# A new order of the setup calls on each engine of an attention kernel

## The chip, the core and the metric

The kernel runs on one core of a Trainium2 chip. The engines are TensorE (PE, matmul and its weight load, PEld), VectorE (DVE), ScalarE (ACT), GpSimd (POOL) and SyncE (SP, which here only issues DMAs; ACT issues DMAs as well). Every engine takes its own instructions strictly in the order in which the program lists them; between engines there are semaphores. The metric is the time of one execution in device microseconds. Before the change: 723.69 us, median of 3 runs (722.16 to 724.40).

## The reference

```python
h = jnp.maximum(_layernorm(x), 0.0)              # x: 4096 x 256
q = h @ Wq.T + bq;  k = h @ Wk.T + bk;  v = h @ Wv.T + bv
a = q @ k.T * (1 / 16) + adj + adj               # 4096 x 4096
out = x + softmax(a, axis=-1) @ v
```

All inputs and the output are fp32. `adj` is 64 MB; it is read once.

## The kernel before

**Precision.** Each fp32 operand of a large product is split into a high and a low fp16 half, and three fp16 products (high x high, high x low, low x high) are summed in PSUM. A high half is a cast on ACT, a low half is a subtraction on DVE or POOL that waits for the high one.

**Scores.** q and k are folded: with M = Wq' Wk (Wq' the transpose) the scores are h M h', scaled, plus bias terms. `project_g(g, c)` makes the query side h M of group g (512 rows of h), feature half c, `evict_g` takes it from PSUM on ACT (one PSUM bank, so the next `project_g` waits for it), `store_g` and `load_g` carry it through a DRAM scratch to `g_pair`. Tiles are taken in pairs (256 rows) against blocks of 1024 keys (a quad q of 4), and each 2 x 2 block product is done with seven products instead of eight (a Strassen-like scheme): `product_1` to `product_7` read the combinations B11, B21, B22 (plain) and T1 to T4 (sums, made by `key_sum_t1` to `t4` on POOL out of `hf`). Their high halves are `high_key(q, i)` on ACT, their low halves `low_key` on DVE or `pool_low_key` on POOL; `LOW_ORDER` and `POOL_LOW_ORDER` say which engine makes which, and the semaphore values are looked up in these lists. DVE reads the results: `scores_11`, `scores_12`, `scores_22` (which also add the scaled adj rows) free the banks `t_ps[n % 2]` for the next product, and `finish_xx` add the second part and take the maximum.

**Values.** `project_v(unit)` (16 units) gives v for 256 rows; `high_v` (ACT) and `low_v` (DVE) write its halves, and `project_v(unit)` waits for `low_v(unit - 1)` since they share a bank. `move_v(g)` brings them with 4 DMAs to `v_sb`.

**Layernorm.** `load_x(g)` brings 512 rows; `statistics(g)` (DVE), `layernorm_factors(g)` (POOL) and four `normalise(g, k)` (ACT) make h; `transpose_h(g, c)` (PE) and `copy_h(g, c)` (ACT) lay it out by features.

**Softmax and weighing.** Per tile `bias` (DVE) gives the maximum, `exponential` (ACT) the weights, `turn` (DVE) and the exchanges `exchange_a` (8 DMAs from SP) and `exchange_b` (8 DMAs from ACT, in four calls of two) transpose them into `xT`; `high(m)` (ACT) and `low(m)` (POOL) split them, and `weigh` (PE) multiplies with `v_sb`. `refill(u, part)` loads the next adj row unit into the ring `rows` of 15 units once the exchange of that unit has landed; `load_rows(r)` does the first 15. `exchange_b(1, ...)` and `exchange_a(1)` wait by `arrival_free` until all products of v and g are through and `move_v(7)` has landed.

**Order.** The setup (up to period 7 of 64) is a list of calls written out by hand on each engine; from period 7 on loops run (`period(n)`), with four weighing parts and seven products in a period. Nothing else sets the order. The profile's line numbers are those of the functions: 1443 is a matmul of projections and weighing, 1504 a score product, 1064 `low_key`, 616 `pool_low_key`, 735 `high_key`, 709 `normalise`, 743 `evict_g`, 750 `high_v`, 1069 `low_v`, 545 `layernorm_factors`, 1046 `statistics`, 556 to 580 the key sums, 778 `exponential`, 789 `exchange_b`, 420 `exchange_a`, 372 the adj rows, 366 the x groups, 409 `move_v`, 391 `store_g`.

## Time and profile before

| | |
|---|---|
| median of 3 runs | 723.69 us |
| profiled execution, its own time | 720.62 us |
| its span, first to last instruction | 718.9 us |
| PE busy | 690.8 us (96%) |
| DVE busy | 603.4 us (84%) |
| ACT busy | 436.4 us (61%) |
| POOL busy | 432.9 us (60%) |
| DMA | 161.06 MB |

The span's clock starts at its first instruction. Busy shares over the whole span mix the setup (about the first 115 us) with the loop, so the stages have to be read apart. In a timeline row the bracket at the end is the idle time of that engine just before the row, and who ended it.

### The profile page before, as it was taken

What the parts mean: (1) busy time and instruction counts of PE and PEld (TensorE: products, weight loads), DVE (VectorE), ACT (ScalarE), POOL (GpSimd) and SP (SyncE); (2) the same over time, 40 slices, a digit from 0 to 9 for tenths busy, and PEclk for the clock granted to TensorE, in tenths of its full rate; (3) what the DMA queues carried; (4) which work ended last, traced back from release to release, by engine and by line L of the source; (5) the groups of instructions that cost most, each with busy time, mean ns of one, the idle gap of its engine ahead of it and who ended that gap; (6) DMA issues with size and microseconds to landing.
All of it is one profiled execution on the core that took longest, in us unless ns stands there. A gap on an engine that the chain in (4) does not pass through costs nothing.

```text
span 718.9 us, 14692 instructions
## 1 busy us (share of the span) xinstructions
PE 690.8 (96%) x4799; PEld 473.4 (66%) x4799; DVE 603.4 (84%) x1282; ACT 436.4 (61%) x732; POOL 432.9 (60%) x436
## 2 busy tenths in 40 slices
PE   4788999999999999999999999999999999999988
PEld 3555555567666667667667666666666666667766
DVE  4889777988897978788888888797988888888896
ACT  4799564665656555656656565656566666656530
POOL 1889603475655667474747556565738475655667
PEclk8799999999999999999999999999999999999999
DMA  8398588998879889898988897888879798878472
GB/s 284 119 279 234 142 223 224 258 252 229 251 207 258 223 230 232 237 240 226 269 208 246 235 254 217 241 216 243 239 217 266 205 256 231 250 217 225 121 187 75
DMA packets 93244, 161.06 MB, mean 224 GB/s; under 512 B 20976, under 2 KB 41840, under 8 KB 93168
## 3 DMA queue, kind: packets, MB, share of 16 engines
q1 hardware_dynamic: 68432, 126.41, 63.9%
q10 hardware_dynamic: 24736, 33.72, 18.3%
q8 instruction: 38, 0.62, 0.4%
q14 instruction: 38, 0.31, 0.2%
HBM read 80.35 MB, written 8.39 MB: 123 GB/s over the span
## 4 chain that ended last, share of the span: by engine, by line
PE 74%; DVE 10%; issue 4%; POOL 3%; DMA 2%; ACT 2%; ACTq 2%; SPq 1%; DVEq 0%; POOLq 0%
PE bank L1443 41%; PE bank L1504 33%; ACTq L789 2%; DVE rows L1128 2%; DVE rows L1101 1%; DMA xT<-rows 1%; DVE top L1137 1%; SPq L420 1%; DVE h_tile L1142 1%; POOL wT L625 1%; DVE stats L1046 1%; DVE rows L1094 1%; DMA rows<-in_x 1%; DMA g_pair<-g_scratch 1%; ACT rows L709 1%
## 5 line engine op out<-in xcount | busy, mean ns | idle before, releaser
L625 POOL TENSOR_TENSOR wT<-xT,wT 128x512 f16<-128x512 f32 x233 | 268.3, 1162 | 209.8 <-ACT wT L807 206.8
L1443 PE MATMUL bank<-v_sb,wT 128*128 128x256 f16 x2796 | 343.0, 273 | 0.2
L1504 PE MATMUL bank<-top,a_op 128*128 128x512 f16 x1344 | 330.8, 379 | 5.5 <-DVE chunk_max L1101 2.3
L1443 PEld LDWEIGHTS bank<-v_sb,wT 128*128 128x128 f16 x2796 | 273.3, 98 | 81.4 <-DVE xy L1191 1.3
L807 ACT CAST wT<-xT 128x512 f16<-128x512 f32 x233 | 139.6, 611 | 124.8 <-PE bank L1443 66.1
L1504 PEld LDWEIGHTS bank<-top,a_op 128*128 128x128 f16 x1344 | 130.6, 98 | 116.0 <-DVE chunk_max L1101 3.6
L778 ACT ACTIVATE rows<-rows,exp_bias,exp_scale 128x1024 f32<-128x1024 f32 x128 | 158.7, 1240 | 65.0 <-issue 31.0
L1101 DVE CUSTOM_DVE_ANT_0 rows<-bank,rows 128x512 f32<-128x512 f32 x256 | 173.6, 680 | 10.7 <-PE bank L1504 2.3
L1128 DVE STREAM_TRANSPOSE rows<-rows 128x1024 f32<-128x1024 f32 x128 | 158.3, 1239 | 5.8 <-ACT rows L778 5.5
L1086 DVE SCALAR_TENSOR_TENSOR rows<-rows,adj_scale,bank 128x512 f32<-128x512 f32 x64 | 47.7, 745 | 41.7 <-PE bank L1504 41.7
L769 ACT ACTIVATE rows<-rows,adj_scale 128x512 f32<-128x512 f32 x64 | 46.2, 722 | 36.0 <-POOL wT L625 20.7
L1079 DVE SCALAR_TENSOR_TENSOR rows<-rows,adj_scale,bank 128x512 f32<-128x512 f32 x64 | 47.5, 742 | 21.9 <-PE bank L1504 21.0
L1094 DVE SCALAR_TENSOR_TENSOR rows<-rows,adj_scale,bank 128x512 f32<-128x512 f32 x64 | 47.2, 737 | 8.4 <-PE bank L1504 8.3
L1443 PE MATMUL bank<-v_sb,top 128*128 128x256 f16 x276 | 31.5, 273 | 2.2 <-DVE top L1137 1.3
L1443 PEld LDWEIGHTS bank<-v_sb,top 128*128 128x128 f16 x276 | 25.6, 98 | 7.9 <-POOL top L625 1.9
L602 POOL TENSOR_TENSOR a_op<-g_pair,a_op 128x512 f16<-128x512 f32 x15 | 17.7, 1183 | 13.0 <-ACT a_op L763 13.0
L592 POOL TENSOR_TENSOR comb<-g_pair 128x128 f32<-128x128 f32 x15 | 6.8, 455 | 29.5 <-DMA g_pair<-g_scratch 29.5
L632 POOL TENSOR_TENSOR xy<-xy,bv_row 128x256 f32<-128x256 f32 x32 | 24.5, 769 | 0.0
L1443 PE MATMUL bank<-top,xT 128*128 128x512 f16 x72 | 19.4, 400 | 4.8 <-ACT xT L743 4.8
L778 ACT ACTIVATION_READ_ACCUMULATOR rows<-rows,exp_bias,exp_scale 128x1 f32 x128 | 23.9, 187 | 0.0
L1142 DVE CUSTOM_DVE_ANT_0 h_tile<-h_tile,wqbk_row,rbias 128x256 f32<-128x256 f32 x32 | 23.2, 726 | 0.1
L1443 PE MATMUL bank<-xT,top 128*128 128x256 f16 x144 | 19.9, 275 | 2.8 <-DVE xT L1069 1.7
(115 smaller groups left out, 478.8 us busy)
## 6 DMA issues: line engine op xcount, KB each, us to landing
rows<-in_adj SPq DMA_DIRECT2D x128, 512.0 KB, 5.9
xT<-rows SPq DMA_DIRECT2D x488, 64.0 KB, 3.2
xT<-rows ACTq DMA_DIRECT2D x488, 64.0 KB, 3.7
rows<-in_x SPq DMA_DIRECT2D x8, 512.0 KB, 5.5
xy<-in_x SPq DMA_DIRECT2D x32, 128.0 KB, 5.8
g_scratch<-xT SPq DMA_DIRECT2D x16, 256.0 KB, 3.4
g_pair<-g_scratch SPq DMA_DIRECT2D x15, 256.0 KB, 4.4
out_y<-xy SPq DMA_DIRECT2D x30, 128.0 KB, 5.7
```

The source lines that it names most:

```text
L625: nc.gpsimd.tensor_tensor(split_piece(m, 1), exchanged(m), split_piece(m, 0), ALU.subtract).then_inc(split_lo, 1)
L769: nc.scalar.activation(part, part, ACT.Copy, scale=adj_scale[:]).then_inc(adj_scaled, 1)
L778: nc.scalar.activation(row, row, ACT.Exp, scale=exp_scale[:], bias=exp_bias[:, p % 2, t:t + 1], accum_out=unit_sum(u, part)).then_inc(expe ...
L807: nc.scalar.copy(split_piece(m, 0), exchanged(m)).then_inc(split_hi, 1)
L1079: nc.vector.scalar_tensor_tensor(part, part, adj_scale[:], t_ps[n % 2][:], ALU.mult, ALU.add).then_inc(t_read[n % 2], 1)
L1086: nc.vector.scalar_tensor_tensor(part, part, adj_scale[:], t_ps[n % 2][:], ALU.mult, ALU.add).then_inc(t_read[n % 2], 1)
L1094: nc.vector.scalar_tensor_tensor(part, part, adj_scale[:], t_ps[n % 2][:], ALU.mult, ALU.add).then_inc(t_read[n % 2], 1)
L1101: return nc.vector.tensor_tensor_reduce(out=row, in0=ps[:], in1=row, scale=1.0, scalar=-3.0e38, op0=ALU.add, op1=ALU.max, accum_out=chunk_ ...
L1128: nc.vector.transpose(unit_row(u, part), unit_row(u, part)).then_inc(turned, 1)
L1142: nc.vector.tensor_tensor_reduce(out=h, in0=h, in1=wqbk_row[:], scale=SCORE_SCALE / H_SCALE, scalar=rbias0[:], op0=ALU.mult, op1=ALU.add, ...
L1443: return nc.tensor.matmul(out_ap, stationary, moving, start=first, stop=last)
L1504: last = nc.tensor.matmul(ps[:], s, mv, start=first and k == 0, stop=k == 2, skip_group_check=True)
```

## The change

It permutes calls within each engine's setup list; the loops and every function stay. One call changes its engine: the low half (0, B21) is made by `pool_low_key` instead of `low_key`. The order of the DMA issues on SP is changed too, and with it the order of the first adj rows (three of them now go ahead of x group 2, and x group 3 after the xy tiles). Blank lines that it removes are left out here, and the lines stand without their indentation.

The lists of which half comes when:

```diff
@@ -50,19 +50,19 @@
...
 HIGH_ORDER = (
-    (0, B11), (0, B21), (0, T1), (0, B22), (0, T3), (0, T2), (0, T4),
-    (1, B11), (1, B21), (1, T1), (1, B22), (1, T3), (2, B11), (1, T2),
-    (1, T4), (2, T1), (2, B21), (2, T3), (3, B11), (2, T2), (2, B22),
+    (0, B11), (0, B21), (0, T1), (0, B22), (0, T2), (0, T3), (0, T4),
+    (1, B11), (1, B21), (1, T1), (1, T3), (1, B22), (2, B11), (1, T2),
+    (1, T4), (2, B21), (2, T3), (2, T1), (3, B11), (2, T2), (2, B22),
     (3, B21), (2, T4), (3, B22), (3, T1), (3, T3), (3, T2), (3, T4),
...
 LOW_ORDER = (
-    (0, B11), (0, B21), (0, B22), (0, T4), (1, B11), (1, B21), (1, B22),
-    (2, B11), (2, B21), (3, B11), (2, B22), (3, B21), (3, B22),
+    (0, B11), (0, B22), (1, B11), (0, T4), (1, B21), (1, B22), (2, B11),
+    (3, B11), (2, B21), (2, B22), (3, B21), (3, B22),
 )
 POOL_LOW_ORDER = (
-    (0, T1), (0, T3), (0, T2), (1, T1), (1, T3), (1, T2), (1, T4),
-    (2, T1), (2, T3), (2, T2), (2, T4), (3, T3), (3, T2), (3, T1),
-    (3, T4),
+    (0, B21), (0, T1), (0, T2), (0, T3), (1, T1), (1, T3), (1, T2),
+    (1, T4), (2, T1), (2, T2), (2, T3), (2, T4), (3, T2), (3, T1),
+    (3, T3), (3, T4),
 )
...
```

SyncE, the order of issue:

```diff
@@ -435,67 +435,67 @@
...
 load_x(1)
+load_rows(0)
+load_rows(1)
+load_rows(2)
 load_x(2)
-load_x(3)
 sp.dma_start(bv_row[:], bv.rearrange("(o d) -> o d", o=1).to_broadcast([P, D])
              ).then_inc(bv_loaded, 16)
-load_rows(0)
-load_rows(1)
 load_xy(0)
...
 load_xy(3)
+load_x(3)
 load_x(4)
-load_rows(2)
+load_rows(3)
+load_rows(4)
 load_x(5)
-load_rows(3)
+load_rows(5)
+load_x(6)
 store_g(0)
-load_x(6)
-load_rows(4)
-load_rows(5)
 move_v(0)
-load_g(1)
 load_x(7)
...
 load_rows(8)
+load_g(1)
+move_v(2)
 sp.wait_ge(h_transposed, 12)
 load_rows(9)
-move_v(2)
 sp.wait_ge(h_transposed, 14)
 load_rows(10)
+move_v(3)
+store_g(1)
 low_keys(sp, 2, B11, B21, B22)
...
 load_rows(12)
-move_v(3)
-store_g(1)
+move_v(4)
 sp.wait_ge(h_transposed, 16)
 load_rows(13)
-move_v(4)
 store_g(2)
...
 store_g(4)
-move_v(6)
 refill(0, 0)
 store_g(5)
+move_v(6)
+move_v(7)
+store_g(6)
 sp.wait_ge(v_moved[0], 64 * (GROUPS // 2))
 load_rows(14)
-move_v(7)
-store_g(6)
-refill(0, 1)
 store_g(7)
 exchange_a(1)
+refill(0, 1)
 refill(1, 0)
+refill(1, 1)
 exchange_a(2)
-refill(1, 1)
...
```

GpSimd:

```diff
@@ -634,52 +634,53 @@
...
 layernorm_factors(1)
+pool_low_key(0, B21)
 key_sum_t1(0)
...
 key_sum_t2(0)
+layernorm_factors(2)
 key_sum_t4(0)
+layernorm_factors(3)
 pool_low_key(0, T1)
-layernorm_factors(2)
+pool_low_key(0, T2)
 pool_low_key(0, T3)
-layernorm_factors(3)
+query_sums(0)
 layernorm_factors(4)
-pool_low_key(0, T2)
-query_sums(0)
 layernorm_factors(5)
...
 layernorm_factors(6)
+key_sum_t2(1)
 pool_low_key(1, T1)
+key_sum_t4(1)
 pool_low_key(1, T3)
-key_sum_t2(1)
-key_sum_t4(1)
 pool_low_key(1, T2)
...
 key_sum_t2(2)
-key_sum_t4(2)
 layernorm_factors(7)
 pool_low_key(2, T1)
+pool_low_key(2, T2)
 pool_low_key(2, T3)
-pool_low_key(2, T2)
+key_sum_t4(2)
 query_sums(1)
+key_sum_t1(3)
 pool_low_key(2, T4)
-key_sum_t1(3)
 key_sum_t3(3)
 key_sum_t2(3)
-pool_low_key(3, T3)
 pool_low_key(3, T2)
 pool_low_key(3, T1)
+pool_low_key(3, T3)
 key_sum_t4(3)
+add_bias(1)
+pool_low_key(3, T4)
 query_low(1, 0)
+add_bias(2)
 query_low(1, 1)
-pool_low_key(3, T4)
-add_bias(1)
-add_bias(2)
-add_bias(0)
 query_sums(2)
 query_low(2, 0)
+add_bias(0)
 low(0)
...
```

ScalarE:

```diff
@@ -820,11 +821,11 @@
...
 copy_h(0, 0)
+normalise(1, 2)
+copy_h(0, 1)
 high_key(0, B11)
-copy_h(0, 1)
+normalise(1, 3)
 high_key(0, B21)
-normalise(1, 2)
-normalise(1, 3)
 act.wait_ge(scales_done, 1)
...
@@ -837,71 +838,71 @@
...
 high_key(0, B22)
+high_v(0)
 act.wait_ge(folded, 2)
...
 nc.scalar.copy(ws_hi[:], fold[:, 3]).then_inc(weights_hi, 1)
+normalise(2, 0)
+high_key(0, T2)
+normalise(2, 1)
 high_key(0, T3)
-high_key(0, T2)
+evict_g(0, 0)
 high_key(0, T4)
-high_v(0)
-normalise(2, 0)
-normalise(2, 1)
-evict_g(0, 0)
 normalise(2, 2)
...
 normalise(3, 0)
-normalise(3, 1)
 evict_g(0, 1)
 copy_h(2, 0)
+normalise(3, 1)
 normalise(3, 2)
-copy_h(2, 1)
 high_key(1, B11)
 high_v(1)
+copy_h(2, 1)
+normalise(3, 3)
+high_key(1, B21)
 high_query(0)
-high_key(1, B21)
-normalise(3, 3)
+high_v(2)
 normalise(4, 0)
-high_v(2)
 normalise(4, 1)
+normalise(4, 2)
 copy_h(3, 0)
-normalise(4, 2)
+normalise(4, 3)
 copy_h(3, 1)
-normalise(4, 3)
+high_v(3)
 high_key(1, T1)
-high_v(3)
+high_key(1, T3)
+copy_h(4, 0)
+scale_adj(0)
 high_key(1, B22)
-copy_h(4, 0)
-high_key(1, T3)
+high_key(2, B11)
 copy_h(4, 1)
+high_v(4)
 normalise(5, 0)
-high_key(2, B11)
 normalise(5, 1)
-high_v(4)
-scale_adj(0)
+high_key(1, T2)
 normalise(5, 2)
-high_key(1, T2)
 normalise(5, 3)
+high_key(1, T4)
 normalise(6, 0)
-high_key(1, T4)
 high_v(5)
...
 normalise(6, 1)
+normalise(6, 2)
 copy_h(5, 1)
-normalise(6, 2)
 normalise(6, 3)
-high_key(2, T1)
+high_key(2, B21)
 scale_adj(1)
-high_key(2, B21)
 copy_h(6, 0)
 high_key(2, T3)
+high_key(2, T1)
 high_key(3, B11)
+high_v(6)
+high_key(2, T2)
+high_key(2, B22)
 copy_h(6, 1)
-high_key(2, T2)
-high_v(6)
-high_key(2, B22)
 normalise(7, 0)
+evict_g(1, 0)
 normalise(7, 1)
-evict_g(1, 0)
 normalise(7, 2)
...
@@ -911,8 +912,8 @@
...
 copy_h(7, 1)
+high_key(3, B22)
 h_for_bias(1)
-high_key(3, B22)
 scale_adj(2)
...
@@ -921,46 +922,46 @@
...
 h_for_bias(2)
+scale_adj(3)
+high_v(9)
+scale_adj(4)
+evict_g(2, 1)
 h_for_bias(3)
-high_v(9)
-scale_adj(3)
 high_key(3, T4)
-evict_g(2, 1)
 high_v(10)
...
 exponential(0, 1)
+evict_g(4, 0)
 high_v(12)
-evict_g(4, 0)
-high_query(2)
 exchange_b(0, 0, 0)
 evict_g(4, 1)
+high_v(13)
 exponential(1, 0)
-high_v(13)
 evict_g(5, 0)
...
 high_v(14)
-scale_adj(4)
 exchange_b(0, 1, 0)
...
 exponential(2, 0)
+exponential(2, 1)
+high_query(2)
+exchange_b(0, 1, 2)
 evict_g(6, 1)
-exchange_b(0, 1, 2)
-exponential(2, 1)
 evict_g(7, 0)
 scale_adj(5)
+exchange_b(1, 0, 0)
 evict_g(7, 1)
...
 scale_adj(6)
-high(1)
-exchange_b(1, 0, 0)
 exchange_b(1, 0, 2)
 exchange_b(1, 1, 0)
+high(1)
 exchange_b(1, 1, 2)
...
```

VectorE:

```diff
@@ -1213,18 +1214,16 @@
...
 last.then_inc(bk_widened, 1)
+statistics(1)
 dve.wait_ge(m_done, 1)
...
                         apply_absolute_value=True)
-statistics(1)
...
@@ -1253,7 +1249,6 @@
...
 low_key(0, B11)
-low_key(0, B21)
 dve.wait_ge(weights_hi, 2)
...
@@ -1271,62 +1266,62 @@
...
                         ).then_inc(weights_lo, 1)
+statistics(3)
+statistics(4)
+low_v(0)
 nc.vector.tensor_tensor(ws_lo[:], fold[:, 3], ws_hi[:], ALU.subtract
                         ).then_inc(weights_lo, 1)
-statistics(3)
-statistics(4)
 low_key(0, B22)
-low_v(0)
 statistics(5)
-low_key(0, T4)
+low_v(1)
 bias_rows()
 low_key(1, B11)
-low_v(1)
-first_query_low()
+low_key(0, T4)
 low_key(1, B21)
 low_v(2)
+first_query_low()
 statistics(6)
+low_v(3)
 scores_11(0)
-low_v(3)
+scores_12(0)
 low_key(1, B22)
-scores_12(0)
 low_key(2, B11)
...
 scores_11(1)
+statistics(7)
 finish_22(0)
-statistics(7)
 scores_12(1)
-finish_21(0)
 low_v(5)
...
 finish_11(0)
-low_key(2, B21)
+finish_21(0)
 finish_12(0)
 low_key(3, B11)
-scores_11(2)
+low_key(2, B21)
 low_v(6)
 low_key(2, B22)
+finish_21(1)
+scores_11(2)
 finish_22(1)
-finish_21(1)
+low_v(7)
+finish_12(1)
 finish_11(1)
-low_v(7)
 low_key(3, B21)
-finish_12(1)
 row_bias(0)
...
 scores_11(3)
+row_bias(1)
 low_key(3, B22)
-row_bias(1)
 scores_22(2)
...
 low_v(8)
+finish_12(2)
 finish_11(3)
-finish_12(2)
 row_bias(2)
+low_v(9)
 scores_12(3)
-low_v(9)
 scores_22(3)
...
@@ -1338,27 +1333,27 @@
...
 finish_21(3)
+scores_11(4)
 bias(1)
-scores_11(4)
+scores_12(4)
+low_v(13)
 turn(1, 0)
-low_v(13)
-scores_12(4)
 scores_11(5)
...
 finish_22(4)
-turn(2, 0)
 scores_12(5)
...
 scores_11(6)
+turn(2, 0)
+scores_12(6)
+finish_22(5)
+finish_11(4)
 turn(2, 1)
-finish_22(5)
-scores_12(6)
-finish_11(4)
 finish_12(5)
...
```

TensorE:

```diff
@@ -1605,26 +1600,26 @@
...
 last.then_inc(small_done, 1)
+project_g(0, 0)
 project_v(0)
-project_g(0, 0)
 project_g(0, 1)
...
 project_v(1)
-project_g(1, 0)
 project_v(2)
 transpose_h(3, 0)
+project_g(1, 0)
 transpose_h(3, 1)
 project_v(3)
+product_1(1)
 product_1(0)
...
 transpose_h(4, 1)
+product_2(0)
+product_6(0)
 project_v(4)
-product_6(0)
-product_1(1)
+product_7(0)
 product_5(0)
-product_7(0)
-product_2(0)
 project_v(5)
...
@@ -1635,19 +1630,19 @@
...
 project_v(6)
+product_2(1)
+product_5(1)
 product_1(2)
-product_5(1)
 product_4(1)
-product_2(1)
 project_v(7)
...
 transpose_h(7, 1)
+product_1(3)
 product_6(2)
-product_1(3)
+project_v(8)
 product_5(2)
-project_v(8)
 product_7(2)
...
@@ -1670,34 +1665,34 @@
...
 project_v(13)
+product_5(4)
 project_g(5, 0)
...
 project_v(14)
+project_g(6, 0)
 product_7(4)
-project_g(6, 0)
 project_v(15)
-product_5(4)
 project_g(6, 1)
...
 product_4(4)
-project_g(7, 0)
 product_3(4)
...
 product_1(6)
-project_g(7, 1)
 product_5(5)
+project_g(7, 0)
 product_6(6)
 product_2(4)
+project_g(7, 1)
 product_3(5)
...
 product_2(5)
+product_4(5)
 product_5(6)
-product_4(5)
-product_4(6)
 product_2(6)
 product_3(6)
+product_4(6)
...
```

## Rows read from the trace of the kernel before

**Rows 1.** stages: window us, busy (x instructions) of PE, PEld, DVE, ACT, POOL; clock, DMA

```profile
...
17.00:72.00 55.00, 43.87 (x263) 28.70 (x264) 50.90 (x126) 48.93 (x96) 48.02 (x48) 0.92 0.74 213
72.00:110.00 38.00, 38.00 (x219) 21.29 (x218) 29.85 (x57) 22.90 (x38) 11.45 (x14) 1.00 0.72 185
110.00:135.00 25.00, 23.20 (x150) 14.08 (x148) 20.21 (x45) 12.72 (x22) 11.60 (x11) 1.00 0.89 231
135.00:700.00 565.00, 562.01 (x4004) 390.34 (x4002) 481.59 (x1002) 344.90 (x568) 343.90 (x343) 1.00 0.86 231
...
```

**Rows 2.** timeline, TensorE: start us, us, line, operation, count [idle before, releaser]

```profile
...
21.91 1.68 PE L1443 MATMUL bank<-xT,top 128*128 128x256 f16 x12
...
29.66 2.74 PE L1443 MATMUL bank<-top,xT 128*128 128x512 f16 x6 [4.78 <-ACT xT L743]
...
71.78 1.47 PE L1504 MATMUL bank<-top,a_op 128*128 128x512 f16 x6 [1.72 <-DVE chunk_max L1101]
...
99.74 1.46 PE L1443 MATMUL bank<-top,xT 128*128 128x512 f16 x6
...
106.86 7.93 PE L1504 MATMUL bank<-top,a_op 128*128 128x512 f16 x36
...
127.42 1.47 PE L1504 MATMUL bank<-top,a_op 128*128 128x512 f16 x6 [1.02 <-DVE rows L1079]
...
```

**Rows 3.** timeline, VectorE

```profile
...
17.21 1.28 DVE L1064 TENSOR_TENSOR top<-rows,top 128x512 f16<-128x512 f32 x2
...
21.03 1.40 DVE L1046 BATCH_NORM_STATS2 stats<-rows 128x6 f32<-128x256 f32 x4
...
23.76 0.16 DVE L1054 TENSOR_SCALAR var_eps<-mean_var 128x4 f32<-128x4 f32 x1
...
35.20 0.79 DVE L1064 TENSOR_TENSOR top<-xT,top 128x512 f16<-128x512 f32 x1 [1.15 <-ACT top L735]
...
45.88 0.75 DVE L1086 SCALAR_TENSOR_TENSOR rows<-rows,adj_scale,bank 128x512 f32<-128x512 f32 x1 [1.63 <-PE bank L1504]
...
67.37 1.67 DVE L1064 TENSOR_TENSOR top<-xT,top 128x512 f16<-128x512 f32 x1
...
```

**Rows 4.** timeline, GpSimd

```profile
...
23.90 1.47 POOL L580 TENSOR_TENSOR wT<-rows,wT 128x512 f32<-128x512 f32 x1
25.33 1.33 POOL L616 TENSOR_TENSOR top<-wT,top 128x512 f16<-128x512 f32 x1
...
67.22 1.27 POOL L564 TENSOR_TENSOR wT<-xT 128x512 f32<-128x512 f32 x1
...
```

**Rows 5.** timeline, ScalarE and its DMA queue (ACTq)

```profile
...
27.94 1.09 ACT L709 ACTIVATE rows<-rows,ln_all 128x256 f32<-128x256 f32 x2 [1.43 <-POOL ln_all L546]
...
88.19 0.61 ACT L763 CAST a_op<-comb 128x512 f16<-128x512 f32 x1
...
101.47 1.16 ACTq L789 DMA_DIRECT2D xT<-rows  x2
102.68 1.24 ACT L778 ACTIVATE rows<-rows,exp_bias,exp_scale 128x1024 f32<-128x1024 f32 x1 [0.70 <-DVE rows L1128]
...
```

**Rows 6.** timeline, SyncE's DMA queue

```profile
...
111.10 6.70 SPq L420 DMA_DIRECT2D xT<-rows  x8
119.71 0.35 SPq L372 DMA_DIRECT2D rows<-in_adj  x1
...
```

**Rows 7.** line 372, issue at 119.71 (row unit 16): time to landing

```profile
...
DMA to landing us min/median/max: 6.0/6.0/6.0
```

**Rows 8.** line 420, exchange_a(0), issues at 87.6 to 92.4: to landing

```profile
...
DMA to landing us min/median/max: 1.9/2.3/2.4
```

**Rows 9.** line 409, move_v(7), issues at 101.0 to 103.0: to landing

```profile
...
DMA to landing us min/median/max: 6.1/6.6/7.3
```

**Rows 10.** line 366, x groups 1 and 2, issues at 3.7 and 4.2: to landing

```profile
...
DMA to landing us min/median/max: 6.0/6.5/7.0
```

**Rows 11.** the page, part 2, the DMA total

```profile
...
DMA packets 93244, 161.06 MB, mean 224 GB/s; under 512 B 20976, under 2 KB 41840, under 8 KB 93168
...
```

## The prediction

> **What bounds the kernel now.** I read the stages first, then the idle time of TensorE (PE), then the other engines at the places where PE waits. The table by stage [rows 1] decides what a change of the setup can be worth: from 135 to 700 us PE is busy 562.01 of 565.00 us, so there PE alone is the bound, and the end moves by what the start of that stretch moves. Before it PE has three stages. From 17 to 72 us it is busy 43.87 of 55.00: 11.1 us idle. From 72 to 110 it is idle for nothing. From 110 to 135 it is idle 1.8 us. So some 13 us are the whole prize. In 17 to 72 us VectorE (DVE) is busy 50.90 of 55 us, so it has 4.1 us to give, and ACT and POOL are as full (48.93, 48.02): the setup is a mesh of three full engines, and PE waits in it.
>
> PE's timeline [rows 2] shows the waits that I work with: 4.78 us before project_g(0,1) at 29.66, for evict_g(0,0); 1.72 us before product_2(3) at 71.78, for finish_11(2) on DVE; 1.02 us at 127.42, for scores_11(8). The middle one is the gauge: it is the last wait before the full stage, so what DVE gains up to finish_11(2), the full stage gains.
>
> All times below are of the profiled execution: span 718.9, 720.62 us with what lies around it. The median of the runs shown is 723.69, 3.07 above; a saving is subtracted from both.
>
> **1. The opening (up to 25 us).** Before PE's second product of keys, the chain on POOL is key_sum_t4(0), pool_low_key(0,T1), then layernorm_factors(2): 1.47 and 1.33 us stand ahead of the factors [rows 4], which ACT's normalise(2,0) then awaits until 27.94 [rows 5]. The statistics of group 2 were done at 23.92 (23.76 + 0.16) [rows 3]. With the factors put ahead of both, they start at about 23.95 instead of 26.65: 2.7 us earlier. ACT gets two casts (high_key(0,T2), (0,T3), about 0.5 us each) in between that it did before, so evict_g(0,0) and PE's wait end some 1.6 us earlier, at about 28.1.
>
> One low half, (0,B21), leaves DVE: two low halves take 1.28 us together at 17.21 [rows 3], so -0.6 on DVE, and +1.2 to 1.3 on POOL (bounds 1.16, the plain rate of the same form, and 1.33 [rows 4]), where POOL sat idle until key_sum_t1(0): hidden. If that cover were gone it would cost 1.3 us at key_sum_t1(0).
>
> On PE project_g(0,0) now precedes project_v(0), whose 12 matmuls started at 21.91 [rows 2]; high_v(0) moves ahead of the casts ms_hi and ws_hi on ACT, so these come at about 25.0, while DVE's statistics(2) ends at 23.9: a new DVE wait before ms_lo. Bounds 0 (PE arrives early enough) and 1.5; I take 0.9, since a part of it is waited out again at low_v(1), which needs ACT. Behind it on DVE stand statistics(3), (4) and low_v(0), and for low_v(0) PE's project_v(1) waits, which comes after the wait of 28.1.
>
> statistics(1) now comes before the first reduction of tops: group 1 lands at 3.7 + 6.0 = 9.7 us [rows 10], and the reduction, some 0.6 us like one call at 17.21, then comes behind; PE turns tops only after transposes(0,0). Cost 0, bounds -0.2 and +0.6.
>
> Loads: rows 0 to 2 (512 KB each) now go ahead of x groups 2 and 3, and four 128 KB xy tiles and bv ahead of group 3. Group 2 landed by 4.2 + 7.0 = 11.2 us [rows 10]; group 3, issued right behind it, I put at 12. At the mean 224 GB/s [rows 11] 1.57 MB add 7.0 us (18.2, needed at 21.03 [rows 3]), and 2.2 MB add 9.8 us (21.8, needed after 25). Cost 0; were the rate half, x(2) would be 4 us late, and that end I keep in the range only as part of the slower tail.
>
> **2. The middle (25 to 72 us).** Swaps among normalise, copy_h, high_key and high_v on ACT, among low_key, low_v, finish and statistics on DVE, key_sum and pool_low_key on POOL, and products on PE keep every call; they can only remove or create waits. DVE had two: 1.15 us before low_key(1,B11) at 35.20 and 1.63 us before scores_12(0) at 45.88 [rows 3]. The first was for ACT, which is now ahead by 0.8 to 1.5 us and so are the casts; DVE also gets low_v(1) and bias_rows first. The second was for PE's product_6(0), which stood behind project_v(4); it now stands before it, and DVE gets there later relative to PE. I take both as gone (bounds: 0 and 2.8 us; walking the new order with these durations leaves DVE short pauses under 0.5 us at low_key(3,B11) and row_bias(0), which the 0.3 us of smaller old pauses roughly pay). Sum for finish_11(2): -0.6 -1.15 -1.63 +0.9 = -2.5 us. product_2(3) starts at about 69.3 instead of 71.78.
>
> One price in this stage is a lock, and it can eat that. At 67.22 POOL runs key_sum_t3(3) for 1.27 us [rows 4]; low_key(3,B22) starts on DVE at 67.37 and lasts 1.67 us [rows 3], against 0.64 a piece at 17.21: it ended 0.6 us after POOL's call did. So DVE stood for the length of POOL's instruction. The Trainium skill (page "SBUF — State Buffer", section "Who interferes with whom") states that a DVE instruction with two SBUF inputs contends with a GpSimd instruction that reads SBUF, and that whoever issues first holds the port for the whole instruction; the trace agrees (1.67 against 0.64). By that rule the half moved to POOL at about 17.1 us would hold up low_key(0,B11), which runs at the same time, for up to 1.2 us, and the 0.6 taken from DVE would be a loss of 0.6: -1.3 in place of -2.5.
>
> **3. The late part (72 to 130 us), in the old times, to be shifted by -2.5.** PE's order from project_v(15) changes: product_5(4) moves from behind project_v(15) to before project_g(5,0), and project_g(7,0) goes behind six products instead of two. project_g(6,1) starts at 99.74 as before [rows 2]; the products are 7.93/12 = 0.65 us each; so project_g(7,0) is due at 99.74 + 1.3 + 6 x 0.65 = 104.9. It needs evict_g(6,1). ACT now does exponential(2,1) (1.24 us and 0.1 for the sum), high_query(2) (two casts, 0.5 each of pitch) and the two exchange issues (1.16) first [rows 5]; the issues move from 101.47 by +0.65 (project_v(15) is later by a product), +1.33, +1.03, -0.5 (an issue runs under the cast ahead of it) and -0.4 (ACT waited there for PE) to about 103.6, end at 104.8, and evict_g(6,1) ends at 105.5. New PE wait: 0.6 us (bounds 0 and 1.3).
>
> Then the queues. exchange_b(1,0,0) is now ahead of evict_g(7,1) and high(0) on ACT; it waits until project_g(7,1) is through (two products later: 109.4) and until move_v(7) has landed. It issues until 110.7, evict_g(7,1) ends 111.3, SP's store_g(7) takes 1.1 us, and exchange_a(1) starts at 112.5 instead of 111.10 [rows 6]. What follows is a fixed chain: 119.71 - 111.10 = 8.6 us to refill(1,0), 6.0 us to the landing of row unit 16 [rows 6, 7], 0.75 for scores_11(8): product_6(8) at 127.85 instead of 127.42 [rows 2]. Today that load (125.7) and ACT's lateness both end near there; it is this load that is late next. The 0.6 at project_g(7,0) lies inside it. Net +0.4. high(0) at about 111.9 plus POOL's low half is ahead of the first weigh at 114.6: no cost.
>
> **Sum:** -2.5 + 0.4 = -2.1 us. Profiled execution 718.5, median 721.6.
>
> **The rivals.**
> (a) The load of unit 16 does not decide, since moving exchange_b(0,1,2) and the refills spreads the transfers, and exchange_b for unit 1 no longer waits for high(1). Then the 1.8 us of waits in 110 to 135 [rows 1] go too: -2.5 - 1.8 = -4.3, 719.4 us. For it: ACT's first exponential of the steady order is freed by about 1 us. Against it: store_g(7) comes later.
> (b) The DVE time comes back as port waits and small pauses: the three engines are over 87% full, and a reordering only changes who waits. Then -1.3 from the lock, half of the 2.8 us of waits stay, and +0.4 remains: about +0.1 to -0.5, say 723.4.
> (c) Slower: SP's queue blocks behind refill(0,0). It now stands ahead of store_g(5), move_v(6) and move_v(7) and waits for exchange_a(0) to land. Now that takes 1.9 to 2.4 us [rows 8], but move_v(7)'s transfers took 6.1 to 7.3 [rows 9]. If the exchange lands as late as those, SP stands 5 us longer, move_v(7) lands at 114 to 117 in old times, exchange_b(1,0,0) holds ACT and with it high(0), and exchange_a(1) starts 4.5 us later still: product_6(8) at 132.3, +4.9 - 2.5 = +2.4, 726.1 us. It decides from a landing of some 4.5 us on.
>
> **How the numbers follow.** A measurement of this kernel tells 0.3%, 2.2 us, from no change. Forecast 0.50 (own range -1.0 to -3.3: 720.4 to 722.7; nearly half of it beyond 2.2 us), (a) 0.15, (b) 0.18, (c) 0.12, other causes 0.05, mostly slower. Faster: 0.24 + 0.15 + 0.05 = 0.44; slower: 0.12 + 0.04 = 0.16; the same: 0.40. The range takes in (a) and (b), and of (c) the milder half: 719.0 to 724.8.
>
> **What would show it.** In the changed profile: evict_g(0,0) near 27.4 and PE's wait ending near 28.1; DVE without waits over 0.5 us from 36 to 68 but one near 24 before ms_lo; finish_11(2) near 68.6; PE idle under 10 us in 17 to 72; a PE wait of about 0.6 us for ACT at project_g(7,0); exchange_a(1) starting near 110.0; product_6(8) near 125.3 after a wait for scores_11(8). The forecast is wrong if product_2(3) starts after 71 or before 68, or if PE gets a wait at the first weigh.

## The result and the profile after

The change made the kernel slower by a third of a per cent: 725.13 us (median of 20 runs, 722.48 to 729.36) against 723.57 (20 runs beside them). The ratio is 1.0031, 95% interval 1.0016 to 1.0045. The forecast was 721.6. The profiled execution of after has a span of 722.4 and its own time is 724.12 us, 1.0 below its median. The one of before (720.62) was 3 us below its median, so the 3.5 us between the two profiles are more than the 1.6 us between the medians, and I read the profiles for what moved and the runs for how much.

The stages of after, same columns and stretches as [rows 1]:

```profile
...
17.00:72.00 55.00, 42.67 (x258) 27.95 (x259) 51.67 (x125) 47.30 (x92) 46.64 (x47) 0.93 0.63 186
72.00:110.00 38.00, 36.90 (x214) 20.47 (x212) 28.84 (x57) 23.56 (x39) 13.21 (x15) 1.00 0.73 194
110.00:135.00 25.00, 23.61 (x150) 14.25 (x149) 20.55 (x48) 12.40 (x20) 11.12 (x10) 1.00 0.89 248
135.00:700.00 565.00, 561.08 (x3986) 388.07 (x3985) 482.12 (x1000) 346.80 (x572) 341.75 (x341) 1.00 0.85 230
...
```

The forecast was PE idle for under 10 us in 17 to 72; it is 12.3 (11.1 before), and 1.1 us of idle are now behind 72 too. DVE is busier, though it makes one low half less. ACT and POOL are less busy. From 110 to 135 PE is idle 1.4 us in place of 1.8.

TensorE's timeline in after, its waits (to be held against [rows 2]):

```profile
...
17.14 1.97 PE L1452 MATMUL bank<-ident,rows 128*128 128x128 f32 x8 [1.18 <-ACT rows L710]
...
28.67 2.74 PE L1438 MATMUL bank<-top,xT 128*128 128x512 f16 x6 [4.54 <-ACT xT L744]
...
35.94 0.50 PE L1438 MATMUL bank<-xT,top 128*128 128x256 f16 x3 [2.15 <-DVE rows L1070]
...
49.26 1.48 PE L1438 MATMUL bank<-xT,top 128*128 128x256 f16 x12 [1.85 <-DVE rows L1070]
...
53.98 1.48 PE L1499 MATMUL bank<-top,a_op 128*128 128x512 f16 x6 [1.07 <-DVE chunk_max L1102]
...
61.64 0.50 PE L1438 MATMUL bank<-xT,top 128*128 128x256 f16 x3 [1.32 <-DVE xT L1070]
...
70.35 1.47 PE L1499 MATMUL bank<-top,a_op 128*128 128x512 f16 x6 [0.93 <-DVE rows L1087]
...
74.21 1.47 PE L1499 MATMUL bank<-top,a_op 128*128 128x512 f16 x6 [1.10 <-DVE chunk_max L1102]
...
129.94 1.47 PE L1499 MATMUL bank<-top,a_op 128*128 128x512 f16 x6 [1.31 <-DVE rows L1080]
...
```

The opening went as forecast: the wait for evict_g(0,0) ends at 28.67 instead of 29.66. Then come six waits on DVE, three of them for low_v (2.15, 1.85 and 1.32 us), the last for finish_11(2), and product_2(3) starts at 74.21, against 71.78 before and 69.3 in the forecast. The first weighing matmul follows: 117.38 instead of 114.63.

VectorE's timeline in after:

```profile
...
17.82 1.56 DVE L1065 TENSOR_TENSOR top<-rows,top 128x512 f16<-128x512 f32 x1
...
23.25 0.98 DVE L1053 TENSOR_SCALAR neg_mean<-mean_var 128x4 f32<-128x4 f32 x1
...
25.39 0.43 DVE L1267 TENSOR_TENSOR wT<-a_op,wT 128x256 f16<-128x256 f32 x1 [1.09 <-ACT wT L844]
...
31.62 1.64 DVE L1065 TENSOR_TENSOR top<-rows,top 128x512 f16<-128x512 f32 x1
...
41.74 0.87 DVE L1053 TENSOR_SCALAR neg_mean<-mean_var 128x4 f32<-128x4 f32 x1
...
44.84 0.75 DVE L1087 SCALAR_TENSOR_TENSOR rows<-rows,adj_scale,bank 128x512 f32<-128x512 f32 x1 [0.92 <-PE bank L1499]
45.51 1.42 DVE L1065 TENSOR_TENSOR top<-xT,top 128x512 f16<-128x512 f32 x1
46.85 1.75 DVE L1065 TENSOR_TENSOR top<-rows,top 128x512 f16<-128x512 f32 x1
...
66.57 1.76 DVE L1065 TENSOR_TENSOR top<-xT,top 128x512 f16<-128x512 f32 x1
...
70.88 1.40 DVE L1143 CUSTOM_DVE_ANT_0 h_tile<-h_tile,wqbk_row,rbias 128x256 f32<-128x256 f32 x1
...
```

GpSimd's timeline in after at three of these places:

```profile
...
17.68 1.16 POOL L616 TENSOR_TENSOR top<-rows,top 128x512 f16<-128x512 f32 x1 [4.36 <-ACT top L736]
...
29.14 3.57 POOL L616 TENSOR_TENSOR top<-wT,top 128x512 f16<-128x512 f32 x3
...
45.22 1.16 POOL L616 TENSOR_TENSOR top<-wT,top 128x512 f16<-128x512 f32 x1
46.34 1.72 POOL L580 TENSOR_TENSOR wT<-xT,wT 128x512 f32<-128x512 f32 x1
...
66.51 1.27 POOL L556 TENSOR_TENSOR wT<-xT 128x512 f32<-128x512 f32 x1 [0.94 <-ACT xT L723]
...
```

The rows come in pairs. (0,B21) runs on POOL from 17.68 to 18.84; low_key(0,B11), started on DVE at 17.82, ends at 19.38: 1.56 us instead of 0.68, and 0.54 behind POOL's end. POOL's three low halves of 29.14 end at 32.71, low_key(0,B22) of 31.62 at 33.26: 0.55 behind. The low half of 45.22 on POOL ends at 46.38, low_key(1,B22) of 45.51 at 46.93: 0.55. key_sum_t4(1) ends at 48.06, low_key(2,B11) of 46.85 at 48.60; key_sum_t1(3) at 67.78, low_key(3,B21) of 66.57 at 68.33. Each time DVE's call does its work only when POOL's is over. The last pair is the kind that the prediction had seen once in before [rows 3, 4]. Even neg_mean, 128 x 4 numbers, takes 0.98 and 0.87 us (0.17 when alone), and row_bias at 70.88 takes 1.40 (0.74). POOL is held too: key_sum_t4(1) at 46.34 took 1.72 us, where its kind takes 1.27 [rows 4].

The price is best read from the groups. VectorE in 17 to 75 us by line and shape (count, busy us, mean ns of one, idle before), low_key and neg_mean, first in before, then in after:

```profile
...
L1064 DVE TENSOR_TENSOR top<-rows,top 128x512 f16<-128x512 f32 x6 | 6.6, 1115 | 0.0
L1064 DVE TENSOR_TENSOR top<-xT,top 128x512 f16<-128x512 f32 x6 | 5.2, 864 | 1.2 <-ACT top L735 1.2
...
L1052 DVE TENSOR_SCALAR neg_mean<-mean_var 128x4 f32<-128x4 f32 x6 | 3.0, 492 | 0.2
...
```

```profile
...
L1065 DVE TENSOR_TENSOR top<-rows,top 128x512 f16<-128x512 f32 x5 | 7.6, 1527 | 0.0
...
L1065 DVE TENSOR_TENSOR top<-xT,top 128x512 f16<-128x512 f32 x6 | 6.5, 1076 | 0.0
L1053 DVE TENSOR_SCALAR neg_mean<-mean_var 128x4 f32<-128x4 f32 x6 | 3.7, 622 | 0.2
...
```

With fewer calls after spends more: the low halves of these two forms are 11.8 us in before (12 calls) and 14.1 in after (11 calls). I call the **excess** what DVE's calls of 17 to 76 us take beyond the duration that the same form has when POOL does not overlap it (low half 0.68, ms_lo and ws_lo 0.41, neg_mean 0.17, row_bias 0.74). It is 8.1 us in before and 11.0 in after. Of before's 8.1, 0.4 lie behind product_2(3), in a row_bias at 74.08; of after's 11.0, nothing does.

### The profile page after: what moved, and what is told of

It is laid out like the page before. It is cut to its first block, busy times and chain, and to the rows that moved or that the text cites. A ratio compares the mean times of both kernels' runs of the same rounds, so it can differ in the third digit from the quotient of the medians.

```text
span 722.4 us, 14698 instructions
## 1 busy us (share of the span) xinstructions
PE 691.0 (96%) x4799; PEld 472.2 (65%) x4799; DVE 606.9 (84%) x1281; ACT 437.1 (61%) x732; POOL 433.2 (60%) x437
## 4 chain that ended last, share of the span: by engine, by line
PE 72%; DVE 12%; DMA 4%; issue 4%; SPq 4%; POOL 3%; ACT 1%; ACTq 0%; DVEq 0%; POOLq 0%
PE bank L1438 40%; PE bank L1499 32%; SPq L420 2%; DVE rows L1129 2%; DVE rows L1102 1%; DVE stats L1047 1%; DVE top L1065 1%; DMA rows<-in_adj 1%; DVE rows L1080 1%; DMA out_y<-xy 1%; DVE h_tile L1143 1%; SPq L409 1%; DVE top L1138 1%; DMA rows<-in_x 1%; DMA v_sb<-xT 1%
## 5 line engine op out<-in xcount | busy, mean ns | idle before, releaser
L1143 DVE CUSTOM_DVE_ANT_0 h_tile<-h_tile,wqbk_row,rbias 128x256 f32<-128x256 f32 x32 | 25.5, 797 | 0.0
```

What stands on the lines that cost most here:

```text
L1143: nc.vector.tensor_tensor_reduce(out=h, in0=h, in1=wqbk_row[:], scale=SCORE_SCALE / H_SCALE, scalar=rbias0[:], op0=ALU.mult, op1=ALU.add, ...
```

## The experiments

Theory 1, formed on this comparison: DVE's time up to finish_11(2) sets the start of the full stage, and the new order gave away there, in DVE calls held by POOL calls, more than it won in waits. Rivals: the half (0,B21) that moved to POOL; DVE's own new list; the late queues; POOL's list by itself. Each ratio is against before, run on the same chip. In the tables the last two columns are DVE's excess and idle time (us) of the profiled execution in 17 to 76; idle time counts the pauses that a timeline shows in brackets. A single profile is compared with care: TensorE's granted clock from 15 to 21 us was 0.50 (its 1.2 GHz level) in before, after, lf_before, lf_after, lf2_before, ps_before and tail_after, and 1.00 (2.4 GHz) in the other seven, so the openings are not alike.

**1. The lock taken away, both orders.** POOL's sixteen key sums and all its low halves (15 in the old order, 16 in the new) become fills of the same tiles, which read nothing (in the lf pair two fills for a key sum and three for a low half, in the lf2 pair two for each). The waits and the order stay, and the kernels leave out what these calls compute.

```diff
-                nc.gpsimd.tensor_tensor(top[:, i, q, 1], source, top[:, i, q, 0], ALU.subtract
-                                        ).then_inc(top_lo_pool, 1)
+                fill_with(top[:, i, q, 1], 3).then_inc(top_lo_pool, 1)   # lf: 3, lf2: 2
```

Old order, three fills. 

> The old order, with the 16 key sums and 15 low halves of GpSimd replaced by fills of the same tiles (zeros, so the keys' sums and these low halves are left out); a fill reads no SBUF, and two or three fills stand for one call, so that GpSimd is busy for about as long. Theory L (lock): VectorE's calls with two SBUF inputs are no longer held up by these calls: low_key lasts 0.68 us throughout (13 calls), and the excess of 7.7 us over plain durations in 17 to 73 us falls under 3. product_2(3), at 71.8 in the old order, comes 1 to 4 us earlier. Rival W (waits by dependency and order): durations of VectorE stay as they are, up to 1.76 us.

New order, three fills. 

> The new order with the same replacement. Theory L: what the new order lost it lost to the lock (excess on VectorE 11.0 us against 7.7 in the old), so without it product_2(3), at 74.2 in the new order, comes before that of the old order under the same replacement, by 0.5 to 2.5 us, and the time is 0 to 3 us below. Rival W: the new order stays behind under the replacement too, by about 2.4 us at product_2(3).

Old order, two fills. 

> The old order with GpSimd's 16 key sums and 15 low halves replaced by fills as in lf_before, but two fills (1.1 us) for every call; three had made a low half 1.6 us where a real one takes 1.15, and that had become a chain of its own (finish and products waiting for GpSimd at 73 to 75 us). Theory L: excess of VectorE near 1 us, product_2(3) between 68 and 71 us, first weighing matmul at 111 to 114.

New order, two fills. 

> The new order with two fills for every call. Theory L: product_2(3) at 69.2 us as with three fills (where it came 5.0 us earlier than with the real calls), and now the first weighing matmul too: 111.5 to 113, before or level with that of the old order under the same replacement. Rival W: 2 us or more behind it.

| kernel | median us | ratio, 95% | first weigh | excess | idle |
|---|---|---|---|---|---|
| before (profiled) | 723.57 | 1 | 114.63 | 8.1 | 3.1 |
| after | 725.13 | 1.0031 (1.0016 to 1.0045) | 117.38 | 11.0 | 3.1 |
| lf_before | 720.86 | 0.9981 (0.9956 to 1.0006) | 114.75 | 1.3 | 9.2 |
| lf_after | 721.25 | 0.9987 (0.9968 to 1.0006) | 114.89 | 1.1 | 9.8 |
| lf2_before | 718.20 | 0.9942 (0.9920 to 0.9963) | 110.81 | 1.0 | 8.7 |
| lf2_after | 718.06 | 0.9928 (0.9908 to 0.9948) | 110.67 | 1.1 | 8.7 |

The 2.75 us between the orders at the first weigh become 0.14 in either pair (the new order 0.14 later in lf, 0.14 earlier in lf2), and the medians agree within 0.4 us. The medians are of 10 runs each for lf and of only 5 and 4 for lf2, and each interval is some 0.2% wide to either side: that is enough to say that the gap of 0.31% is not seen, and not that it is exactly nothing. VectorE's groups in lf2_after, the same stretch as above:

```profile
...
L1065 DVE TENSOR_TENSOR top<-xT,top 128x512 f16<-128x512 f32 x6 | 4.1, 686 | 0.7 <-ACT top L736 0.7
L1065 DVE TENSOR_TENSOR top<-rows,top 128x512 f16<-128x512 f32 x5 | 3.4, 683 | 0.0
...
L1053 DVE TENSOR_SCALAR neg_mean<-mean_var 128x4 f32<-128x4 f32 x6 | 2.1, 355 | 0.2
...
```

Every low half is back at 0.68 us, beside a POOL that is still filling the same tiles: it is POOL's reading that holds these calls, not POOL's being at work. neg_mean, with a single SBUF input, is less held than before but not free: 0.36 in the mean, against 0.17 alone. The fills are a little short (two take 1.1 us, a low half 1.16, a key sum 1.27), so lf2 also relieves POOL; three are too long (1.63), and in both lf kernels POOL itself becomes late near 75 us (PE waits 0.83 us for it in lf_after, 0.82 in lf_before). TensorE's timeline in lf_after:

```profile
...
69.17 1.47 PE L1499 MATMUL bank<-top,a_op 128*128 128x512 f16 x6 [0.17 <-DVE chunk_max L1102]
...
74.78 0.81 PE L1499 MATMUL bank<-top,a_op 128*128 128x512 f16 x3 [0.83 <-POOL top L544]
...
```

product_2(3) starts there at 69.17, the forecast's 69.3. But in lf_before it starts at 69.34 and without a wait, so the lead of 0.5 to 2.5 us that I expected of the new order there is 0.17 (0.68 in the lf2 pair, 67.29 against 67.97, and gone at the first weigh). Without the lock DVE has 9 us to spare, and neither order is measurably ahead of the other.

**2. The half (0,B21) back on DVE,** all else new.

```diff
             layernorm_factors(1)
-            pool_low_key(0, B21)
...
             low_key(0, B11)
+            low_key(0, B21)
```

> The new order throughout, but the low half (0, B21) back on VectorE behind (0, B11). Theory L: low_key(0,B11) loses the 0.9 us that it stood behind GpSimd's call (1.56 to 0.68 us), VectorE gets 0.6 us more work: no change within 0.5 us at product_2(3), the time within 1 us of the new kernel. Rival: the move itself is the cause of the loss, then the time returns to the old one, -2.2 us.

725.20 us, ratio 1.0036 (1.0019 to 1.0052); product_2(3) at 74.02, first weigh 117.70, excess 11.0, idle 3.8. The stretch of 17.82 went (0.9 us) and another came: ms_lo at 24.32 took 0.86 us more than its 0.41. Moving the half is not the cause of the loss, and giving it back does not remove it.

**3. DVE's old list on the new order of the rest.**

```diff
-            statistics(1)
             dve.wait_ge(m_done, 1)
...
-            scores_12(0)
             low_key(1, B22)
+            scores_12(0)
...
```

> The new order on all engines but VectorE, which has its old order (without low_key(0,B21)). If VectorE's own order is the cause (ws_lo and low_key(0,B22) now behind low_v(0), statistics(7) ahead of finish_22(0), low_key(3,B22) behind row_bias(1)), product_2(3) comes at 72 or before and the time is 2 us below the new kernel. If the cause lies in how GpSimd's and ScalarE's calls fall against VectorE's, it stays at 74 or comes later, and the time stays or rises.

725.55 us, 1.0029 (1.0006 to 1.0052); first weigh 120.02. Excess 7.8, about as in before, but idle 7.4: DVE's old list waits for engines that now come in another order (PE then waits 2.98 us at 38.85). So DVE's new list does fit the other four lists, and what it pays is the excess; the old one pays in waits. DVE's list is not at fault by itself.

**4. POOL's new list alone** on the old order of the rest, (0,B21) with it.

```diff
+            pool_low_key(0, B21)
             key_sum_t1(0)
             key_sum_t3(0)
             key_sum_t2(0)
+            layernorm_factors(2)
             key_sum_t4(0)
-            pool_low_key(0, T1)
-            layernorm_factors(2)
...
```

> The kernel before with POOL's new order alone, (0,B21) on POOL included; the other four engines keep their old order except that DVE leaves (0,B21) out. Theory 1 (no one engine's list is at fault, what counts is which DVE calls meet a POOL call): DVE's stretch beyond its plain durations changes by up to 2 us either way from 7.0, ratio 0.998 to 1.003, and the first weigh follows DVE's account. Rival (POOL's new list makes the loss by itself, on any partner): stretch near 9.9 us, first weigh near 117.4, ratio 1.003 or above.

724.11 us, 1.0016 (0.9996 to 1.0036): not told from no change. Excess 8.4, idle 3.0, product_2(3) at 71.88, first weigh 114.73. PE's wait for evict_g(0,0) fell from 4.78 to 4.00 as the earlier factors promise; but DVE's six neg_mean calls now take 3.3 us more than when alone, where it was 1.9 (one of them alone 1.29 us, at 51.84). POOL's list does not make the whole loss by itself.

**5. The held calls read PSUM.** A low half subtracts the fp16 tile from an fp32 copy in SBUF. That fp32 tile was copied out of PSUM, where it still stands until the next transposes. Five low halves of DVE now take it from there (three of them were held in after, by 2.6 us together, and two in before, by 2.1) and so have one SBUF input; the transposes that reuse the bank wait for them. Nothing of the computation changes.

```diff
+FROM_PSUM = ((0, B22), (1, B11), (2, B11), (3, B11), (3, B22))
...
+                if (q, i) in FROM_PSUM:
+                    source = hT_ps[0 if i == B11 else 1][:]
                 dve.wait_ge(top_hi, high_keys(q, i))
                 nc.vector.tensor_tensor(top[:, i, q, 1], source, top[:, i, q, 0], ALU.subtract
...
+                last_of = (((g - 1) // 2, (B11, B21)[c]) if g % 2 else (g // 2 - 1, B22 if c else None))
+                if last_of in FROM_PSUM:
+                    pe.wait_ge(top_lo, LOW_ORDER.index(last_of) + 1)
```

New order. 

> The new order, all work done; but five low halves on VectorE, (0,B22), (1,B11), (2,B11), (3,B11) and (3,B22), take the fp32 operand from the PSUM bank of the transposes instead of from its copy hf, so that they read one SBUF input only; transpose_h of the next group in that bank waits for them. Theory L: these five last 0.68 us even beside GpSimd's calls; (0,B22), (2,B11) and (3,B11) had 0.96, 1.07 and 0.55 us on top: VectorE gains up to 2.6 us, product_2(3) comes at 71.5 to 73 instead of 74.2, the time falls by 1 to 2.6 us to about that of the kernel before. Rival W, or if a call waits for something else than the port: durations stay, no gain, and up to 1 us lost by the new wait of TensorE.

Old order. 

> The old order with the same five low halves read from PSUM. Theory L: (2,B11) had 1.08 and (3,B22) 0.99 us on top, so VectorE gains 2.0 us before product_2(3), which comes at 69.7 to 71 instead of 71.8; the time falls by 0.8 to 2 us against the kernel before and this is the fastest of the kernels that do all work. Rival: no gain.

Old order, (0,B21) and (1,B21) as well. 

> The old order with seven instead of five low_key calls that read PSUM: (0,B21) and (1,B21) as well. Theory 1: each of the two no longer can be held by POOL; (0,B21) was not stretched in the old order, (1,B21) by 0.4 us, while the transposes that reuse the bank now wait for them (0.2 to 0.5 us each), so no gain over ps_before: ratio 0.996 to 0.998. Rival (any operand in PSUM helps): ratio below 0.996.

| kernel | median us | ratio, 95% | first weigh | excess | idle |
|---|---|---|---|---|---|
| ps_after | 722.86 | 0.9994 (0.9968 to 1.0021) | 113.65 | 6.2 | 4.0 |
| ps_before | 721.18 | 0.9969 (0.9954 to 0.9985) | 114.14 | 5.5 | 4.3 |
| ps6_before | 720.81 | 0.9974 (0.9953 to 0.9996) | 112.79 | 5.6 | 4.9 |

VectorE's timeline in ps_after around 31 us, where after had 1.64 us:

```profile
...
29.03 0.55 DVE L1054 TENSOR_SCALAR neg_mean<-mean_var 128x4 f32<-128x4 f32 x1
...
29.56 0.68 DVE L1073 TENSOR_TENSOR rows<-bank,rows 128x512 f16<-128x512 f32 x1
30.16 0.78 DVE L1275 TENSOR_TENSOR wT<-a_op,wT 128x256 f16<-128x256 f32 x1
30.87 0.68 DVE L1068 TENSOR_TENSOR top<-bank,top 128x512 f16<-128x512 f32 x1
...
```

and GpSimd's in ps_after at the same time:

```profile
...
28.40 3.56 POOL L617 TENSOR_TENSOR top<-wT,top 128x512 f16<-128x512 f32 x3
...
```

Three of POOL's low halves run from 28.40 to 31.96. low_key(0,B22) at 30.87 lies beside them and takes 0.68 us, low_v(0) at 29.56, which reads a PSUM bank, 0.68 too; neg_mean at 29.03 and ws_lo at 30.16, with SBUF inputs alone, are held (0.55 and 0.78). In ps_after the excess fell by 4.8 us, more than the 2.6 that the five calls had: calls that were not touched met other POOL calls (neg_mean at 52.28 took 0.96 us in after; its counterpart, at 51.40, takes 0.24). ps_before beats both kernels by an interval that leaves out 1; ps6_before is no better than it, since the two halves added were hardly held in the old order. This is the version to keep: 0.3% faster than before with one operand changed.

Both orders gain about the same from it (0.31% and 0.37%). The gap between them, 0.31%, is 0.25% with the five calls freed, though in the excess it is only 0.7 us where it was 2.9. The two do not go together here: by the excess the gap in time should have shrunk to a quarter. In the profiles ps_after is even ahead at product_2(3) (70.48 against 71.26) and at the first weigh. The intervals of the two ratios overlap (0.9968 to 1.0021, 0.9954 to 0.9985), so either the spread of the runs hides it or something besides the excess sets the gap; that is not settled.

**6. The late queues of before on the new order.** SyncE's list from exchange_a(0) on and ACT's exchange_b(1,0,0) go back to their old places.

```diff
             refill(0, 0)
             store_g(5)
...
+            refill(0, 1)
             store_g(7)
             exchange_a(1)
-            refill(0, 1)
             refill(1, 0)
-            refill(1, 1)
             exchange_a(2)
+            refill(1, 1)
...
-            exchange_b(1, 0, 0)
             evict_g(7, 1)
+            exchange_b(1, 0, 0)
```

> The changed kernel with SyncE's late order of before (refill(0,1) ahead of store_g(7) in the queue, refill(1,1) behind exchange_a(2), move_v(6) and store_g in their old places) and exchange_b(1,0,0) back behind evict_g(7,1) on ACT; the order up to 110 us stays the new one. Theory 1 (the loss of the change is the lock between DVE and POOL in 17 to 72 us, and the late queues cost some tenths more): the wait for scores_11(8), 1.31 us in the changed kernel, falls below 0.5, the first weigh stays later than the old one by about 2 us (116.5 against 117.4 and 114.6), the time is about 1 us below the changed kernel: 724.0, ratio 1.0015. Rival (the late queues make the loss): the ratio is 1.000 or below.

With the five PSUM operands too. 

> The same late order, and the five low_key calls of DVE that stretched most beside POOL read their fp32 operand from PSUM instead of SBUF, as in the earlier kernel ps_after. There the first weigh was at 113.65 and a wait of 2.1 us stood before scores_11(8) for the adj rows. Theory 1: that wait falls below 0.5, first weigh about 112.5, time about 721 us, ratio 0.997. Rival: another wait (ACT's high halves) takes its place and nothing is gained over ps_after: ratio 0.9995.

tail_after: 726.27 us (7 runs), 1.0056 (1.0034 to 1.0078), first weigh 116.98, excess 11.0; ps_tail_after: 722.50, 1.0002 (0.9982 to 1.0021). The wait for scores_11(8) was expected to fall from 1.31 us to under 0.5. It did not; TensorE's timeline in tail_after:

```profile
...
128.49 0.61 PE L1438 MATMUL bank<-v_sb,wT 128*128 128x256 f16 x4 [0.19 <-POOL wT L625]
130.13 1.47 PE L1499 MATMUL bank<-top,a_op 128*128 128x512 f16 x6 [1.03 <-DVE rows L1080]
...
```

What went is DVE's wait for the adj rows (1.13 us in after). In its place DVE now comes late from a wait of 2.51 us for ACT's exponential, as in before (2.68), where PE's wait was 1.02. And no time came back: the expected 724.0 is below the interval of what was measured (725.2 to 728.4). The new late queues are not the loss; whether they gain 0.2%, as these two runs hint, is not settled, since after's own interval overlaps. ps_tail_after was expected at 721 and gained nothing over ps_after; the wait that was to fall from 2.1 to under 0.5 was still 1.02, again with DVE waiting for ACT ahead of it (2.78 us): the rival that its expectation names.

ps_after and ps_tail_after run the same lists until exchange_a(0), past 85 us, so they show how far two single profiles of one program stand apart. project_g(0,0) on TensorE in ps_after:

```profile
...
20.62 1.45 PE L1441 MATMUL bank<-top,xT 128*128 128x512 f16 x6
...
```

and in ps_tail_after:

```profile
...
21.74 2.22 PE L1441 MATMUL bank<-top,xT 128*128 128x512 f16 x6
...
```

The same six matmuls took 1.45 us in one and 2.22 in the other, at a granted clock of 1.00 in both, so project_v(0), which now stands behind them, ran at 23.80 instead of 21.91. ACT's high_v(0) waited for it, DVE's ms_lo for the casts behind high_v(0) (1.82 us instead of 0.40), and the first weigh came at 117.20 instead of 113.65, while the excess is 6.2 and 6.1. One profile does not tell 2 us from nothing at the first weigh; what is said of the orders' times above rests on the medians, and what is said of held calls on rows that repeat in several profiles.

## Why the prediction was wrong

Its own steps, one by one.

- **Factors put ahead, evict_g(0,0):** right. PE's wait ended at 28.67 (28.1 forecast) though all of the opening stood 0.6 us later: low_key(0,B11) began at 17.82, not 17.21. no_b21 and tail_after, with almost the same opening, began it at 16.83 and 17.34, so this shift looks like scatter.
- **(0,B21) off DVE, -0.6:** the call went, and its lock took 0.9 at low_key(0,B11). The prediction had this as its doubt ("a loss of 0.6"); with 1.56 - 0.68 against 0.6 saved it came out at +0.3. no_b21 shows that the end does not depend on it.
- **The wait before ms_lo, 0.9:** measured 1.09 at 25.39.
- **Loads at no cost:** right. After its first group of x, DVE waited for no load of x up to 76 us.
- **DVE's two old waits gone, -1.15 and -1.63:** the first went. The second became 0.92 at 44.84, and small ones of 0.39 and 0.31 came. The bracketed idle time up to finish_11(2) fell from 3.14 to 2.71 us; with the pauses too short for a bracket it fell from 4.07 to 3.26, so -0.8 where the sum had -1.9 with ms_lo's wait in it.
- **"Sum for finish_11(2): -0.6 -1.15 -1.63 +0.9 = -2.5 us": this is the step that failed.** Measured: -0.6 (call) -0.8 (idle) +3.3 (excess up to there, 11.0 against 7.7) +0.6 (opening) = +2.5, and product_2(3) at 74.21 instead of 71.78 is +2.4. The term that was left out is the excess, and the waits gave less than half of what was counted on. The prediction saw the lock at 67.37, priced it at the one call that changed its engine, and treated every other duration as fixed. But a reordering of three lists sets anew which of some twenty DVE calls with SBUF inputs alone meet which of some thirty POOL calls, and before held 8.1 us of such stretch that no wait showed. The Trainium skill (page "SBUF — State Buffer", section "Who interferes with whom") says that a DVE instruction with two SBUF inputs contends with a GpSimd instruction that reads SBUF and not with one that only writes it. For the low halves experiments 1 and 5 agree (0.68 us in lf2_after beside fills and in ps_after with a PSUM operand, up to 1.76 us otherwise). neg_mean has one SBUF input and was held all the same, so part of the excess is not of this kind.
- **Rival (b)** named the mechanism, port waits that eat the gain, but bounded it at 1.3 us and so ended at "about +0.1 to -0.5". It was bounded by one call; the measured price is 3.3 us. Its own terms do not give that total either: -1.3, +1.4 for half of the 2.8 us of waits and +0.4 make +0.5, or about 724.2, which would have been nearer.
- **Rival (a)**, the late waits going too: no. PE is idle 1.4 us in 110 to 135 where it was 1.8, and its wait at 129.94 comes, through DVE, from the load of unit 16.
- **PE wait of 0.6 for evict_g(6,1) at project_g(7,0):** not there. The prediction let the two DMA issues of exchange_b(0,1,2) take 1.16 us between high_query(2) and evict_g(6,1). ACT's rows in after (ACTq: its DMA queue):

```profile
...
102.74 0.51 ACTq L790 DMA_DIRECT2D xT<-rows  x1
102.85 1.24 ACT L779 ACTIVATE rows<-rows,exp_bias,exp_scale 128x1024 f32<-128x1024 f32 x1
103.28 0.61 ACTq L790 DMA_DIRECT2D xT<-rows  x1
...
104.09 1.23 ACT L779 ACTIVATE rows<-rows,exp_bias,exp_scale 128x1024 f32<-128x1024 f32 x1
...
106.34 0.68 ACT L744 ACTIVATE xT<-bank,g_bias 128x512 f32<-128x512 f32 x1
...
111.69 1.16 ACTq L790 DMA_DIRECT2D xT<-rows  x2
112.94 0.69 ACT L744 ACTIVATE xT<-bank,g_bias 128x512 f32<-128x512 f32 x1 [2.74 <-DVE rows L1129]
...
```

  These two issues are listed behind exponential(2,0), (2,1) and high_query(2), yet they went out at 102.74 and 103.28, while the first of these, at 102.85, had hardly begun. So the order that the kernel's description gives to every engine held among ACT's activations, and not between them and the DMA issues. The two lay under the work listed ahead of them and stood in nobody's way: evict_g(6,1) began at 106.34, and ended at 107.02, ahead of PE's project_g(7,0), which ran from 107.35 without a pause. The forecast had this call of PE due at 104.9 and ACT done at 105.5, 107.3 and 107.9 with after's delay of 2.4: PE was on time, ACT 0.9 us early. exchange_b(1,0,0) at 111.69 and evict_g(7,1) behind it at 112.94 are in the order that the prediction gave.
- **The queues, +0.4:** exchange_a(1) started at 114.79, 2.6 us before the first weigh, where before it was 3.5 us before it (111.10 against 114.63) [rows 6]; so it came 0.9 us late for its place where 1.4 were forecast. The wait for the load of row unit 16 came as said: DVE waited 1.13 us for the adj rows and PE 1.31 at 129.94, where it was 1.02 [rows 2]. Product_6(8) stands 12.56 us behind the first weigh, 12.79 before. Net -0.2, not +0.4.
- **Rival (c)**, SP blocked behind refill(0,0): no. move_v(7) was issued at 104.88, and what exchange_a(1) stood behind was store_g(7) at 113.66, which waited for evict_g(7,1) as the sum had it. The slower result has nothing of its mechanism.

SyncE's queue in after, for the last two points:

```profile
...
104.88 2.78 SPq L409 DMA_DIRECT2D v_sb<-xT  x4
...
113.66 0.97 SPq L391 DMA_DIRECT2D g_scratch<-xT  x2
114.79 6.21 SPq L420 DMA_DIRECT2D xT<-rows  x8
...
```

What the runs show together, in order of DVE's excess:

| kernel | excess | idle | ratio |
|---|---|---|---|
| lf2_before, lf2_after | 1.0, 1.1 | 8.7, 8.7 | 0.9942, 0.9928 |
| ps_before, ps6_before | 5.5, 5.6 | 4.3, 4.9 | 0.9969, 0.9974 |
| ps_after, ps_tail_after | 6.2, 6.1 | 4.0, 5.9 | 0.9994, 1.0002 |
| no_dve | 7.8 | 7.4 | 1.0029 |
| before | 8.1 | 3.1 | 1 |
| only_pool | 8.4 | 3.0 | 1.0016 |
| after, no_b21, tail_after | 11.0, 11.0, 11.0 | 3.1, 3.8, 3.1 | 1.0031, 1.0036, 1.0056 |

Except for no_dve, whose loss is idle time, and the lf pair with its slow POOL (excess 1.3 and 1.1, 0.998 and 0.999), the ratio rises with the excess, some 0.1% (0.7 us) for each microsecond from end to end. Within that it is loose: ps_after lies 1.9 us of excess below before at the same time, and tail_after 0.25% above after at the same excess. Shown is that without POOL's reads no gap between the orders is seen, and that taking an SBUF input away from five calls speeds up either. Shown for one profile of each is that the excess outweighs the other terms up to product_2(3). That the excess alone makes the whole 0.31% is the reading that fits best, and is not shown: the fills also relieve DVE as a whole, so the lf and lf2 pairs would be equal too if any shortage of DVE time, the excess among others, were the cause. To settle it the calls of the new order would have to be freed one at a time; that was not tried, and neither was the new list of ACT or of PE alone.
